# One-core sequence layer on Trainium2: attention's output weights split by head into contiguous 16-bit rows, and a new order at the opening of the state-space stage

## What is computed

```python
x = _layernorm(x + mamba2(x))     # state-space layer: 128 heads of 64, state 128, 8 groups, chunks of 128 tokens
x = _layernorm(x + sinq(x))       # 512x512 linear layer, its weights dequantised from 4-bit integers
x = _layernorm(x + attention(x))  # 32 query heads of 128, 8 key/value heads, rotary, causal softmax
x = _layernorm(x + swiglu(x))     # silu(x @ gate.T) * (x @ up.T) @ down.T, int8-range weights, 1376 inner
...
out = jnp.einsum('bkgts,bksd->bkgtd', attn, v)                 # in attention
out = out.reshape(B, NUM_HEADS, T, HEAD_DIM).transpose(0, 2, 1, 3).reshape(B, T, NUM_HEADS * HEAD_DIM)
return jnp.einsum('bto,ho->bth', out, Wo)                      # the output weights that the change is about
```

## Time and profile before

| | |
|---|---|
| median of 3 executions | 2475.66 us (2474.8 to 2475.94) |
| the profiled execution, its own time | 2476.66 us |
| its span | 2474.6 us |
| PE busy | 2373.2 us, 96% of the span |
| DVE busy | 1791.4 us, 72% |
| ACT busy | 1591.7 us, 64% |
| POOL busy | 1255.2 us, 51% |

### The profile page before, as it was taken

How to read it: one execution, slowest core, us unless ns; L and a number is a source line. 1 busy time by engine, 2 the same in 40 slices (tenths; PEclk the granted TensorE clock), 3 DMA queues, 4 the chain that set the end, 5 groups by cost and what they waited for, 6 DMA issues and landing times. The chain is left out here.

```text
span 2474.6 us, 48904 instructions
## 1 busy us (share of the span) xinstructions
PE 2373.2 (96%) x15424; PEld 1359.8 (55%) x15624; DVE 1791.4 (72%) x3234; ACT 1591.7 (64%) x3327; POOL 1255.2 (51%) x1002
## 2 busy tenths in 40 slices
PE   6999999999999999999999998789999999999897
PEld 3555555555555555555555555445555555555443
DVE  5677787787777777787777776577777777778522
ACT  7676776776776776776776775365556555656422
POOL 4465555555556556556556569443434343454223
PEclk8999999999999999999999999989999999999899
DMA  7343343343343343343343441320110110100000
GB/s 249 101 132 108 115 130 107 115 131 108 113 133 105 115 133 106 114 134 105 113 134 105 131 146 50 138 89 1 43 44 1 44 44 1 43 18 1 1 0 34
DMA packets 113827, 218.79 MB, mean 88 GB/s; under 512 B 9632, under 2 KB 43040, under 8 KB 111360
## 3 DMA queue, kind: packets, MB, share of 16 engines
q1 hardware_dynamic: 113536, 215.28, 27.0%
HBM read 212.10 MB, written 3.15 MB: 87 GB/s over the span
## 5 line engine op out<-in xcount | busy, mean ns | idle before, releaser
L989 ACT ACTIVATE E<-wq,cst 128x128 f32<-128x128 f32 x1024 | 311.7, 389 | 3.0 <-PEq L298 3.0
L256 DVE SCALAR_TENSOR_TENSOR xc<-bank,taps,xc 128x511 f32<-128x511 f32 (+2 forms) x384 | 284.9, 742 | 35.5 <-ACT xc L243 18.0
L1919 POOL TENSOR_TENSOR qT<-qT,qrot 128x512 f32<-128x512 f32 x64 | 81.2, 1269 | 370.1 <-DVE qrot L1809 370.1
L1282 POOL TENSOR_TENSOR acc<-acc,sq 128x512 f32<-128x512 f32 x112 | 173.1, 1545 | 183.3 <-ACT sq L1001 183.3
L1273 POOL TENSOR_TENSOR xw<-xt,wdec 128x384 f32<-128x384 f32 x128 | 106.4, 831 | 294.1 <-DVE xt L1124 150.7
L1166 DVE SCALAR_TENSOR_TENSOR u<-xc,D,bank 128x512 f32<-128x512 f32 x128 | 95.6, 747 | 205.8 <-PE bank L814 194.2
L1105 DVE TENSOR_TENSOR E<-E,cbm 128x1024 f32<-128x1024 f32 x128 | 242.8, 1897 | 0.8
L59 PE MATMUL bank<-xhi,wx 128*128 128x512 f16 x640 | 242.8, 379 | 0.0
L60 PE MATMUL bank<-xlo,wx 128*128 128x512 f16 x640 | 242.8, 379 | 0.0
L61 PE MATMUL bank<-xhi,wx 128*128 128x512 f16 x640 | 242.6, 379 | 0.0
L1268 POOL TENSOR_TENSOR ecs<-ecs,xcC 128x768 f32<-128x768 f32 x128 | 234.1, 1829 | 0.4 <-POOLq L298 0.4
(11 more groups left out here) (240 smaller groups left out, 6315.0 us busy)
## 6 DMA issues: line engine op xcount, KB each, us to landing
wq<-cs_rows SPq DMA_DIRECT2D x128, 512.0 KB, 4.1
ecs<-ecs_rows SPq DMA_DIRECT2D x128, 384.0 KB, 3.6
wx<-in_w_xbc SPq DMA_DIRECT2D x80, 256.0 KB, 2.7
wz<-in_w_z SPq DMA_DIRECT2D x64, 256.0 KB, 2.7
wo<-in_w_o SPq DMA_DIRECT2D x64, 256.0 KB, 4.0
wq<-in_wq SPq DMA_DIRECT2D x8, 1024.0 KB, 5.8
awo<-in_wo SPq DMA_DIRECT2D x8, 1024.0 KB, 5.0
wkv<-in_wkv SPq DMA_DIRECT2D x8, 512.0 KB, 3.9
```

The lines of the kernel that those rows point to most:

```text
L256: self.nc.vector.scalar_tensor_tensor(out=dst[:, d:T], in0=self.k.bank[bank][:, 0:T - d], scalar=self.taps[:, bass.ds(g, 1), b, j, 3 - d:4 ...
L989: ins = nc.scalar.activation(E[t.i % 4][:, h, c], sc.csr[t.i % 2][:, h, c * P:(c + 1) * P], ACT.Relu, scale=-1.0, bias=head(sc.cst, t, c, h))
L1282: nc.gpsimd.tensor_tensor(acc[t.b][:], acc[t.b][:], sq[:], ALU.add).then_inc(acc_done, 1)
```

## The change

1. Output weights of attention. Instead of two 1 MB buffers there is one raw buffer of one head (`awo_raw`, 128x512, 256 KB), and two pairs of contiguous 16-bit buffers `awohi` (bfloat16) and `awolo` (float16). In each slot of b = 0, POOL makes the rest of that head (TENSOR_TENSOR, `rest_of_wo`) and copies its lead (`lead_of_wo`), after `qT` (and `kT`) and before the slot's split. The splits of `awo` in slots 6 and 7 and `split_first_wo` are gone. SP loads one head at a time, each waiting for the two semaphores of the head before (`wo_ok`, `wo_lead`). PE waits for those two before a unit's first output, and `product` reads the contiguous halves.
2. Opening of the mixer. On PE `turn_B` of tile 0 goes into another bank (`OUT[3]`), without the wait on `cbm_done`, ahead of the gate. ACT takes decays(0), `bt`, exponentials(0), gate(0), decays(1), decays(2); and in the first slot decays(3) come after the silu. SP's load of the other groups' `taps` moves ahead of the `cs_rows` stores of the first sequence.
3. The buffers of one LayerNorm live in the mixer's memory only. No instruction changes with that.

```diff
                     sc.load_wz(sp, 0, j)
+                sp.dma_start(sc.taps[:, 1:NG], io["conv"][:, 1:NG]).then_inc(loaded, 16)
...
                 sc.load_wo(sp, 0, 0)
-                sp.dma_start(sc.taps[:, 1:NG], io["conv"][:, 1:NG]).then_inc(loaded, 16)
...
-                def turn_B(t):
-                    pe.wait_ge(cbm_done, t.u + 1)
-                    bank = k.bank[ring_bank(1 - t.b, USE_BT)]
+                def turn_B(t, bank):
...
                     products_CB(t)
+                    turn_B(t, OUT[3])
                     gate(t)
-                    turn_B(t)
...
                     if nu and s.i == 6:
-                        turn_B(nu)
+                        pe.wait_ge(cbm_done, nu.u + 1)
+                        turn_B(nu, k.bank[ring_bank(1 - nu.b, USE_BT)])
...
                     act.wait_ge(bt_ready, t.u + 1)
-                    nc.scalar.copy(bt[t.b][:], k.bank[bank][:, 0:(CH - 1) * P].rearrange("p (c n) -> p c n", n=P)).then_inc(bt_done, 1)
+                    nc.scalar.copy(bt[t.b][:], bank[:, 0:(CH - 1) * P].rearrange("p (c n) -> p c n", n=P)).then_inc(bt_done, 1)
...
                     decays(tile_at(0, 0))
-                    decays(tile_at(0, 1))
+                    turned_B(tile_at(0, 0), OUT[3])
...
                     gate(tile_at(0, 0))
-                    turned_B(tile_at(0, 0), ring_bank(1, USE_BT))
+                    decays(tile_at(0, 1))
...
                         sc.tap(act, q, ring_bank(s.b, x_use(s)), sc.xc[t.i % 4], t.g, t.b, 2 + t.i)
-                        decays(t)
+                        if not (isinstance(g, int) and g == 0 and m == 0):
+                            decays(t)
...
                         sc.silu(act, q, sc.xc[t.i % 4])
+                    if isinstance(g, int) and g == 0 and m == 0:
+                        decays(t)
...
                     if nu and s.i == 6:
-                        turned_B(nu, ring_bank(s.b, USE_BT))
+                        turned_B(nu, k.bank[ring_bank(s.b, USE_BT)])
...
 T_AT = [(5, 0), (6, 0), (5, 0), (5, 256)]
-W_PIECES = 5
+W_PIECES = 3
...
         S = k.sem
-        self.tabs_in, self.w_in, self.wo_in = S("tabs_in"), [S(f"aw_in{i}") for i in range(2)], [S(f"awo_in{i}") for i in range(2)]
-        self.w_ok = S("aw_ok")
+        self.tabs_in, self.w_in, self.wo_in = S("tabs_in"), [S(f"aw_in{i}") for i in range(2)], S("awo_in")
+        self.w_ok, self.wo_ok, self.wo_lead = S("aw_ok"), S("awo_ok"), S("awo_lead")
...
     def other_buffers(self, ctx):
-        def sb(name, shape):
-            return self.k.sb(name, shape, F32, ctx)
+        def sb(name, shape, dt=F32):
+            return self.k.sb(name, shape, dt, ctx)
...
         self.wkv.append(sb("wkv1", [P, KT, 2 * P]))
-        self.wo = [sb(f"awo{i}", [P, QH, HS]) for i in range(2)]
+        self.wo_raw = sb("awo_raw", [P, HS])
+        self.wo_hi = [sb(f"awohi{i}", [P, QH, HS], BF16) for i in range(2)]
+        self.wo_lo = [sb(f"awolo{i}", [P, QH, HS], F16) for i in range(2)]
...
-    def load_wo(self, sp, g, s):
-        sp.dma_start(self.wo[s][:], self.io["wo"][bass.ds(g, 1)].squeeze(0)).then_inc(self.wo_in[s], 16)
+    def load_wo(self, sp, g, h):
+        if not (isinstance(g, int) and g == 0 and h == 0):
+            sp.wait_ge(self.wo_ok, g * QH + h)
+            sp.wait_ge(self.wo_lead, g * QH + h)
+        sp.dma_start(self.wo_raw[:], self.io["wo"][bass.ds(g, 1), :, h].squeeze(0)).then_inc(self.wo_in, 16)
...
+    def lead_of_wo(self, s, h):
...
+        self.nc.gpsimd.tensor_copy(self.wo_hi[s][:, h], lead(self.wo_raw[:])).then_inc(self.wo_lead, 1)
...
+    def rest_of_wo(self, pool, g, s, h):
+        pool.wait_ge(self.wo_in, (g * QH + (h + 1)) * 16)
+        self.nc.gpsimd.tensor_tensor(self.wo_lo[s][:, h], self.wo_raw[:], lead(self.wo_raw[:]), ALU.subtract).then_inc(self.wo_ok, 1)
...
-        w = self.wkv[s][:] if i == 0 else (self.wq if i < 3 else self.wo)[s][:, 0:2] if i % 2 else (self.wq if i < 3 else self.wo)[s][:, 2:4]
+        w = self.wkv[s][:] if i == 0 else self.wq[s][:, 2 * i - 2:2 * i]
...
-    def split_first_wo(self, pool):
-        pool.wait_ge(self.wo_in[0], 16)
-        self.split(0, 3)
-        self.split(0, 4)
...
-        wq, wkv, wo = aw.wq, aw.wkv, aw.wo
+        wq, wkv, wo_hi, wo_lo = aw.wq, aw.wkv, aw.wo_hi, aw.wo_lo
         cos, sin = aw.cos, aw.sin
-        tabs_in, w_in, wo_in, w_ok = aw.tabs_in, aw.w_in, aw.wo_in, aw.w_ok
+        tabs_in, w_in, w_ok = aw.tabs_in, aw.w_in, aw.w_ok
...
                 aw.load(sp, 1, 1)
-                aw.load_wo(sp, 1, 1)
...
-                    if not (isinstance(g, int) and g in (0, NG - 1)):
-                        sp.wait_ge(proj_ready, ring(g, 0, QH - 1, 1)[0] + 1)
-                        aw.load_wo(sp, g + 1, 1 - s)
+                    for h in range(QH):
+                        if not (isinstance(g, int) and g == 0 and h == 0):
+                            aw.load_wo(sp, g, h)
...
                         x = slice(t * P, (t + 1) * P)
-                        w = wo[s][:, h]
-                        mm = product(nc, k.bank[bank][:, :], (ohi[b][:, h, x], olo[b][:, h, x]), (lead(w), rest(w)),
+                        mm = product(nc, k.bank[bank][:, :], (ohi[b][:, h, x], olo[b][:, h, x]), (wo_hi[s][:, h], wo_lo[s][:, h]),
...
                                     if what == 0:
-                                        pe.wait_ge(w_ok, W_PIECES * (g + b))
+                                        pe.wait_ge(aw.wo_ok, QH * (g + b))
+                                        pe.wait_ge(aw.wo_lead, QH * (g + b))
...
                 add_q(2, 2)
-                aw.split_first_wo(pool)
...
                                 add_k(g * NB + b + 1, 1 - b)
-                            i = (None, None, 0, 1, 2, None, 3, 4)[QH * b + h]
+                            if b == 0:
+                                aw.rest_of_wo(pool, g, s, h)
+                                aw.lead_of_wo(s, h)
+                            i = (None, None, 0, 1, 2, None, None, None)[QH * b + h]
...
                                     pool.wait_ge(w_in[1 - s], 32 * (p + 1 + s))
-                                if i == 3:
-                                    pool.wait_ge(wo_in[1 - s], 16 * (p + 1 + s))
```

More of the change, by code:

```diff
@@ L1362, with __init__ @@
 class LayerNorm:
-    def __init__(self, k, name):
+    def __init__(self, k, name, ctx=None):
         self.k, self.nc = k, k.nc
[L1368 to L1371, removed]
+        self.stats = k.sb(name + "stats", [P, TT, 6], F32, ctx)
+        self.mv = k.sb(name + "mv", [P, TT, 2], F32, ctx)
+        self.rstd = k.sb(name + "rstd", [P, TT], F32, ctx)
+        self.shift = k.sb(name + "shift", [P, TT], F32, ctx)
         S = k.sem
@@ L2219, in program @@
         k.mhalf = k.sb("mhalf", [P, 1])
-        k.norms = [LayerNorm(k, f"n{b}_") for b in range(NB)]
+        k.norms = [LayerNorm(k, "n0_")]
         with ExitStack() as early:
@@ L2223, in program @@
             with ExitStack() as mix:
+                k.norms.append(LayerNorm(k, "n1_", mix))
                 sc = Scan(k, io, aw, mix)
```

## The result

The changed kernel takes 2482.56 us (median of 11 executions, 2478.53 to 2487.18), beside 2475.94 us for the kernel before in the same session (11 executions, 2474.8 to 2478.32). The ratio is 1.0025, with a 95% interval of 1.0016 to 1.0034: slower by 0.25%. Forecast were 2482.9 us and, as likeliest, slower. The profiled execution has a span of 2480.7 us, 6.1 more than before.

The account below looks back on a forecast made before the run. PE's own work (9.75 us a slot) or the chain through `nmx` (9.11 plus its lateness) bounds attention. Terms -5.7 - 1.5 + 3.2 + 11.6 + 3.0 - 3.4 = +7.2 on 2475.66 give 2482.9 us; range 2461 to 2489.

Parts of the forecast that it names:

- (a): Attention's output matmuls: contiguous moving rows take 379 instead of 388 ns, 0.11 us an output, -5.7 us for 52 outputs.
- (b): First unit of attention: without `split_first_wo` the first `nmx` is no longer held, -1.5 us.
- (c): Group 0, slots 2 and 3: the split, begun ahead of `nmx`, makes it 1.6 us late in each, +3.2 us.
- (d): Groups 1 to 6, 12 slots with splits: late `nmx` lengthens each from 9.75 to 10.7 us, +11.6 us.
- rival 1: Split slots: rest and copy take over 1.74 us together, `nmx` passes ahead of the split, 2464.2 us; chance 0.31.
- (e): Attention slots without splits: `qlo` or casts, now later, hold `nmx`, mainly in first slots, +3.0 us.
- (f): Opening of the mixer: waits of PE's states and second scan shrink, a later `wo` gives some back, -3.4 us.
- rival 2: Output matmuls don't get faster and the other terms stay: +12.9, 2488.6 us; chance 0.04.

Follow-up runs that it names:

- the strided experiment: The late weights, but rest and lead of a head written into the halves of 32-bit words, every second 16-bit element: 2470.91 us, ratio 0.9981.
- The late weights: The changed kernel, but POOL makes rest and lead of a head at the slot's start, behind `qlo` and ahead of `qT`: 2463.93 us, ratio 0.9948.

## Why the prediction was right

That the sum came within 0.4 us is in part luck: the stretch from the mixer's fourth scan to attention and that behind the last scores scatter by 2.6 and 4.1 us between the profiled executions, and the two effects of PE's clock in group 0 cancel. The terms that can be read slot by slot stand firmer.

(a) Right: 380 instead of 388 ns, 7.0 us for all outputs by the strided experiment, which is 64 x 0.11.

(b) Right: 1.47 us.

(c) and (d) Right in mechanism and in size. The copy's price, which no row showed, was 0.57 us instead of 0.62, inside the bounds; the lateness was 1.54 instead of 1.6, and the slots of (d) 10.60 to 10.75 us but for one of 10.91. The bound mattered more than the value: anything from 0.56 to 0.72 put the split ahead of `nmx`. That the split's place decides, and that 0.27 us more work in front of it would have helped, was the condition of rival 1. Two experiments let `nmx` pass, one by more work and one by another order; both gave 14 to 15 of the 18.7 us that lie between forecast and rival, and kept most of (e). The late weights, which take most of (e) away too, came to 2463.93 us against the rival's 2464.2. One reading was loose: what I called a gap between two POOL instructions is none by the recorded ends. There `nmx` starts 0.14 us ahead of the split's end and, like the held ones, ends 0.03 behind it; being held so briefly costs nothing that can be seen.

(e) Right in sum. In groups 1 to 5 the first slots are 15.10 to 15.18 us long, against 14.94 to 15.05 with a free `nmx` in the version with the late weights; the slots with casts in groups 6 and 7 lost 0.33 to 0.45 each. In group 0 the first slot lost 0.4 us beside the clock's share, where I had 0.21.

(f) The sum was right, 3.4 against 3.78 by attention's first scores, and ACT got `wo` at 76.40 as forecast. Two sizes inside it were off. I gave 2.5 us to the states' end of waiting and 2.2 to the gate. By the second scan's distance from the stage's first PE instruction, 24.68 us before, 22.93 with the decays in their old place and 20.59 in the changed kernel, the first move gave 1.8 and the second 2.3: ACT was done with the second gate only 1.8 us earlier, so that PE's wait there grew from 2.24 to 4.92 us. By the third scan only 0.8 us of the first move alone is left (37.05 us before, 36.23), since PE ran at the lower clock after that wait. And the late `wo`, to which I gave back 1.3 of 4.7 us, did not hold the third scan in the changed kernel: PE, at a granted clock of 0.75 from 68.0 to 74.8 us, came to it without a wait, 0.14 us behind the gate's end. In the version with the late weights the clock was 1.00 there, and PE waited 1.14 us for that gate.

The range of the forecast's own sum, 2478 to 2489, is wider than its terms give: with the bounds of the copy and of the opening they come to about 2479 and 2486.

Rival 1 failed on the price of the copy, rival 2 on the matmuls' 380 ns, as the rows had it.

## What to carry to other kernels

A POOL instruction that had begun 0.2 us ahead of the small `nmx` held it to its own end; one that began 0.07 us behind it did not. Ask of every instruction that is put on POOL what it puts in front of the small DVE instruction that others wait for, and read from the trace when that one arrives: work behind it was free here, the same work ahead of the split cost 14 us. A stage in which one engine is 99% busy (PE, 598.1 of the 606.3 us from item 8 to item 63 in the kernel before) still has a chain just below, here 0.6 us below; a change that makes the busy engine's work shorter narrows that gap as well. And where PE waits, look at its clock too: in group 0 stretches at the lower clock cost up to 1.7 us, in places that moved from version to version.

## What was not expected of the hardware

More work made the kernel faster: 28 additional POOL instructions took some 14 us away. In that version a 128x512 rest takes 1.04 us and a 128x256 one 0.61, a copy 0.61 and 0.40: by an estimate from the two sizes about 0.19 us of each do not depend on the size, so that halves are dear where there is no such edge. In the strided version the 128x512 copy, written with a step of two, takes 0.77 us instead of 0.61.

The changed kernel's executions spread over 8.7 us (2478.53 to 2487.18), those of the kernel before over 3.5 and those of the version with the late weights over 2.9 in five. That the late `nmx` and PE's waits in twelve more slots are the cause is not shown. The record speaks rather against it: the strided version, which has neither, spreads over 7.4 us in ten, and the kernel before over 6.3 in another session.
